# The first cross-attention rewritten: 32-column products, splits on ScalarE and GpSimd, a new order of work in each tile

## What is computed

```python
q = layernorm(x)                         # rows of 512, mean and variance of each
# B = 8 batches, channels 256, length 512, 8 heads of 32 channels
qk  = einsum('bhdq,bhdl->bhql', qh, kh) / sqrt(32)
sm  = softmax(qk, axis=-1)
ret = einsum('bhql,bhdl->bhdq', sm, vh)
x   = x + gamma * ret                    # k and v are both ctx
```

## Time and profile before

| what | value |
|---|---|
| median of three executions | 2164.12 us (2162.57 to 2165.21) |
| the profiled execution: its own time | 2165.63 us |
| the profiled execution: its span | 2163.8 us |
| first masked product of tile 0, of tile 15 | 45.38 us, 489.10 us |
| first instruction of VectorE in the next block | 526.78 us |
| mean granted TensorE clock | 0.957 |

### The profile page before, as it was taken

One profiled execution on the slowest core, in us unless ns is written; L12 is line 12 of the kernel. 1 busy time (PEld: TensorE's weight loads), 2 busy tenths in 40 slices (PEclk: granted clock), 3 DMA queues, 4 the chain that ended last, 5 costly groups with the idle time before them and its releaser, 6 DMA issues. The chain is left out here.

```text
span 2163.8 us, 33174 instructions
## 1 busy us (share of the span) xinstructions
PE 1887.0 (87%) x10911; PEld 876.8 (41%) x11054; DVE 1692.2 (78%) x3042; ACT 1262.2 (58%) x2016; POOL 794.7 (37%) x681
## 2 busy tenths in 40 slices
PE   3998888896699999799398999999999997869998
PEld 0433333332244443354253444444444443324444
DVE  6799999998826637388688999999999994684443
ACT  2666666654534625144146999999999994521211
POOL 3112222212514515000202888888888883000000
PEclk9999999998899999899698999999999998889999
DMA  6754334402000000110001555555555656000000
GB/s 136 231 115 87 72 67 84 84 9 81 0 0 1 0 0 1 65 33 29 25 0 40 108 108 104 108 108 108 108 105 109 108 106 219 5 1 20 20 20 20
DMA packets 343369, 143.06 MB, mean 66 GB/s; under 512 B 307408, under 2 KB 315600, under 8 KB 342096
## 3 DMA queue, kind: packets, MB, share of 16 engines
q1 hardware_dynamic: 343248, 141.51, 29.5%
HBM read 70.15 MB, written 4.19 MB: 34 GB/s over the span
## 5 line engine op out<-in xcount | busy, mean ns | idle before, releaser
L1385 ACT ACTIVATE a_prob<-a_psS,a_bias,q_scale 128x1024 uint8<-128x1024 f32 x512 | 610.6, 1209 | 26.6 <-PE a_psS L1278 25.6
L1314 DVE TENSOR_REDUCE a_tops<-a_psM 128x1 f32<-128x512 f32 x1024 | 622.7, 681 | 2.0 <-PE a_psM L1268 0.4
L1364 POOL CAST a_wide<-a_pairs 128x2048 int16<-128x2048 uint8 x256 | 481.0, 1894 | 97.3 <-DMA a_pairs<-a_prob 84.8
L1268 PE MATMUL a_psM<-KT,QO 128*128 128x512 bf16 x968 | 353.5, 387 | 16.0 <-DVE a_tops L1314 10.3
L1278 PE MATMUL a_psS<-KT,QO 128*128 128x512 bf16 x967 | 292.9, 380 | 6.6 <-ACT a_prob L1385 3.6
L561 PE MATMUL psO<-prob,vs 128*128 128x512 f32 x512 | 267.2, 604 | 25.3 <-ACT prob L361 20.6
L1290 PEld LDWEIGHTS a_psO<-V,a_wide 128*128 128x128 f16 x4096 | 175.3, 96 | 144.3 <-DVE QO L1327 23.0
L361 ACT ACTIVATE prob<-psT 128x512 f32<-128x512 f32 x256 | 150.7, 595 | 127.1 <-PE psT L549 113.4
L675 POOL TENSOR_TENSOR g_sum<-g_sum 128x512 f32<-128x512 f32 x88 | 126.9, 1442 | 196.9 <-DVE g_sum L740 196.9
L1290 PE MATMUL a_psO<-V,a_wide 128*128 128x32 bf16 x4096 | 181.3, 177 | 20.3 <-DVE QO L1327 15.6
L849 PE MATMUL g_psY<-raw_dn,g_hT 128*128 128x512 f32 x352 | 162.2, 622 | 26.2 <-DVE raw_dn L700 15.8
(11 more groups left out here) (194 smaller groups left out, 2892.4 us busy)
## 6 DMA issues: line engine op xcount, KB each, us to landing
xs<-in_x SPq DMA_DIRECT2D x64, 256.0 KB, 4.7
cs<-in_ctx SPq DMA_DIRECT2D x64, 256.0 KB, 7.7
KT<-in_w SPq DMA_DIRECT2D x2, 4096.0 KB, 21.0
raw_gu<-in_gu SPq DMA_DIRECT2D x4, 1408.0 KB, 17.4
vs<-in_ctxT SPq DMA_DIRECT2D x64, 64.0 KB, 2.2
k_cT<-in_ctxT SPq DMA_DIRECT2D x16, 256.0 KB, 2.7
a_pairs<-a_prob SPq DMA_TRANSPOSE x256, 2.7
out<-x_sb SPq DMA_DIRECT2D x16, 256.0 KB, 2.0
```

What stands on the lines that cost most here:

```text
L1268: pe.matmul(psM[n % NM][:, :], QOf[:, i * P:(i + 1) * P], KTf[:, keys:keys + 512], start=True, stop=True).then_inc(shown, 1)
L1314: v.reduce_max(tops[i // JOIN % NB][:, i % JOIN, c:c + 1], psM[n % NM][:, :], AX.X).then_inc(topped, 1)
L1364: pool.tensor_copy(wide[i % NV][:, :, :, :].rearrange("p k c q -> p k (c q)"), both).then_inc(widened, 1)
L1385: act.activation(prob[i % NP][:, k * HK:(k + 1) * HK], psS[g % NS][:, :], ACT.Exp, scale=q_scale[:, i:i + 1], bias=bias[i // JOIN % NB][:, ...
```

## The change

`mix_rows` is written anew, with nothing else touched.

- **Weighing** goes from one fp32 product of 128 stationary columns per unit to two of 32: for each chunk c, four products (one for each head) into partitions 32h to 32h + 31 of `psO` with the head's 32 rows of ctx, then four into the same partitions of a new bank `psE` with ones. A tile has 32 of them, in four bursts. `collect` is then two reads of 128 partitions for a tile in place of eight of 32. `prob` is a ring of 8. ctx for weighing is fetched in one transfer without the ones.
- **Masking**: the maxima's parts of all units stand in one tile of 51 rows (`PARTS`), turned by one transpose and copied once. In `tscore` the product of L549 becomes four products of 128 columns, each with its own 51-row stationary from the constant `less`, which is built once at the start.
- **Splits**: the queries' normalisation goes from VectorE to ScalarE (`normalise`, four of 128x512), and both operands are split the same way: ScalarE masks two halves (`cut_keys`, `cut_queries`, 128x1024 each), GpSimd subtracts head by head. The Newton step, and the second and third part of the maxima, go to GpSimd, as short instructions.
- **Order**: in a tile TensorE issues two `score` of j + 1 after each of the first eight `tscore` (n = 0 to 7, before 6 to 13). VectorE does the 16 maxima of j + 1 first, with nothing between, then the inversions of j - 1, the row copy of j + 1, and last the statistics of j + 3. ScalarE does the start of the roots of j + 3 after its last exponential. `psS` has three banks, the operands three buffers, everything is prepared a tile earlier (`LEAD = 3`), and the hardware loops are unrolled. Half of the decoding of the FP4 weights comes a tile earlier on VectorE.

The diff, cut to its core:

```diff
-    FIRST = 6
     NU = HT * LC
+    RING = 2 * HT
+    NP1 = NU + 1
+    PARTS = 3 * NP1
+    LEAD = 3
...
+        psS = [pb(f"psS{i}", [P, DM], F32) for i in range(3)]
         psT = [pb(f"psT{i}", [P, DM], F32) for i in range(2)]
...
-        psM = pb("psM", [3, NU, P], BF16)
...
+        psO, psE = pb("psO", [P, DM], F32), pb("psE", [P, DM], F32)
+        psM = pb("psM", [PARTS, P], BF16)
...
+        def turns(steps):
+            for j in range(-LEAD, NT):
+                steps(j)
...
+            for j in range(NT):
+                if has(j + 3):
+                    fetch_x(j + 3)
+                if has(j + 2):
+                    fetch_c(j + 2)
+                if has(j + 1):
+                    fetch_v(j + 1)
+                if j == 0:
+                    sp.dma_start(x_sb[:, 0:2, :], x_tiles[:, 0:2, :]).then_inc(x_loaded, 16)
+                if j == 1:
+                    sp.dma_start(x_sb[:, 2:, :], x_tiles[:, 2:, :]).then_inc(x_rest, 16)
+                if 2 <= j < 2 + CH:
+                    g = j - 2
+                    sp.dma_start(env["raw_gu"][:, g, :],
+                                 gu_in[g * P:(g + 1) * P, :]).then_inc(env["gu_loaded"][g], 16)
...
+                own = Counter(pool, root_own, 6 * j)
+                if j:
+                    pool.wait_ge(normed, j)
+                pool.wait_ge(varied, HT * (j + 1))
+                own.link(pool.tensor_scalar(ve[:, :], mv[b][:, :, 1], LN_EPS, None, ALU.add))
+                pool.wait_ge(guessed, j + 1)
+                own.link(pool.tensor_tensor(tmp[:, :], guess[b][:, :], guess[b][:, :], ALU.mult))
+                own.link(pool.tensor_tensor(tmp[:, :], tmp[:, :], ve[:, :], ALU.mult))
+                own.link(pool.tensor_scalar(tmp[:, :], tmp[:, :], -0.5, 1.5, ALU.mult, ALU.add))
+                if j >= 2:
+                    pool.wait_ge(normal, HT * (j - 1))
+                own.link(pool.tensor_tensor(ys[b][:, :], guess[b][:, :], tmp[:, :], ALU.mult))
+                own.link(pool.tensor_tensor(moved[:, :], mv[b][:, :, 0], ys[b][:, :], ALU.mult))
+                pool.tensor_scalar(away[b][:, :], moved[:, :], -1.0, None, ALU.mult).then_inc(normed, 1)
...
+            def keys(j):
+                if j >= 3:
+                    pool.wait_ge(tscored, NU * (j - 2))
+                for h in range(HT):
+                    pool.wait_ge(k_cut, 2 * j + h // 2 + 1)
+                    pool.tensor_tensor(ks[j % 3][:, h, :], cs[j % 2][:, h, :], k_sub[:, h, :],
+                                       ALU.subtract).then_inc(k_ready, 1)
+            def queries(j):
+                if j >= 3:
+                    pool.wait_ge(tscored, NU * (j - 2))
+                for h in range(HT):
+                    pool.wait_ge(q_cut, 2 * j + h // 2 + 1)
+                    pool.tensor_tensor(qs[j % 3][:, h, :], xs[j % 3][:, h, :], q_sub[:, h, :],
+                                       ALU.subtract).then_inc(q_ready, 1)
+            def split(j):
+                b = j % 2
+                own = Counter(pool, part_own, 2 * j)
+                if j:
+                    pool.wait_ge(parts_ready, j)
+                pool.wait_ge(part_hi, j + 1)
+                own.link(pool.tensor_tensor(rrest[:, :], rmax[b][:, 0:NU], rparts[b][:, 0, 0:NU], ALU.subtract))
+                own.link(pool.tensor_copy(rparts[b][:, 1, 0:NU], rrest[:, :]))
+                pool.tensor_tensor(rparts[b][:, 2, 0:NU], rrest[:, :], rparts[b][:, 1, 0:NU],
+                                   ALU.subtract).then_inc(parts_ready, 1)
...
+            def steps(j):
+                if has(j - 2):
+                    finish(j - 2)
+                if has(j + 2):
+                    keys(j + 2)
+                if has(j + 1):
+                    split(j + 1)
+                if has(j + 2):
+                    queries(j + 2)
+                if has(j + 3):
+                    roots(j + 3)
...
+                act.activation(k_sub[:, half, :], cs[j % 2][:, half, :], ACT.Copy,
+                               scale=k_lo[:, :]).then_inc(k_cut, 1)
...
+            def normalise(j, h):
+                if h == 0:
+                    act.wait_ge(normed, j + 1)
+                act.activation(xs[j % 3][:, h, :], xs[j % 3][:, h, :], ACT.Identity, scale=ys[j % 2][:, h:h + 1],
+                               bias=away[j % 2][:, h:h + 1]).then_inc(normal, 1)
+            def cut_queries(j, k):
+                half = slice(2 * k, 2 * k + 2)
+                act.wait_ge(normal, HT * j + 2 * k + 2)
+                if j:
+                    act.wait_ge(q_ready, HT * (j - 1) + 2 * k + 2)
+                act.activation(q_sub[:, half, :], xs[j % 3][:, half, :], ACT.Copy,
+                               scale=q_lo[:, :]).then_inc(q_cut, 1)
...
+            def collect(j):
+                b = j % 2
+                act.wait_ge(pv_done, NU * (j + 1))
+                if j >= 2:
+                    act.wait_ge(mixed_s, j - 1)
+                    act.wait_ge(added, j - 1)
+                act.activation(weighed[b][:, :], psO[:, :], ACT.Copy, scale=gamma[:, :]).then_inc(o_read, 1)
+                act.activation(e_sums[b][:, :], psE[:, :], ACT.Copy).then_inc(o_read, 1)
+            def steps(j):
                 for n in range(NU):
...
+                    if has(j):
+                        exp(j, n)
+                    if n in (0, 1) and has(j + 2):
+                        cut_keys(j + 2, n)
+                    if n == HT - 1 and has(j - 1):
+                        collect(j - 1)
+                    if n == NU - 1 and has(j + 3):
+                        roots(j + 3)
+                    if 6 <= n < 6 + HT and has(j + 2):
+                        normalise(j + 2, n - 6)
+                    if n in (10, 11) and has(j + 2):
+                        cut_queries(j + 2, n - 10)
...
+            def steps(j):
+                if has(j + 1):
+                    maxima(j + 1)
+                if has(j - 1):
+                    invert(j - 1)
+                if has(j + 1):
+                    maxima_rows(j + 1)
+                if has(j + 3):
+                    statistics(j + 3)
+                if has(j - 2):
+                    after(j - 2)
+                if j == NT - 2:
+                    move(0)
+                    move(1)
+                    mask(0)
+                    mask(1)
+                if j == NT - 1:
+                    move(2)
+                    move(3)
+                    scale(0)
+                    scale(1)
+                    mask(2)
+                    mask(3)
+                    scale(2)
+                    scale(3)
...
+            def tscore(j, n):
+                c, h = n // HT, n % HT
+                g = NU * j + n
+                if g >= 2:
+                    pe.wait_ge(exped, g - 1)
+                out = psT[n % 2]
+                pe.matmul(out[:, :], ks[j % 3][:, h, c * P:(c + 1) * P], qs[j % 3][:, h, :],
+                          start=True, stop=False)
                 if n == 0:
...
+                    pe.wait_ge(mrow_ready, j + 1)
+                for q in range(LC):
+                    mm = pe.matmul(out[:, q * P:(q + 1) * P], less[:, h * LC + q, :], mrow[j % 2][:, :],
+                                   start=False, stop=(q == LC - 1))
+                mm.then_inc(tscored, 1)
...
+            def weigh(j, c):
                 if c == 0:
...
+                    pe.wait_ge(v_in_s[j % 2], 16 * (j // 2 + 1))
+                    if j:
+                        pe.wait_ge(o_read, 2 * j)
+                pe.wait_ge(exped, NU * j + HT * (c + 1))
+                for h in range(HT):
+                    pe.matmul(psO[h * D0:(h + 1) * D0, :], vs[j % 2][:, c, h * D0:(h + 1) * D0],
+                              prob[:, (c * HT + h) % RING, :], start=(c == 0), stop=(c == LC - 1))
+                for h in range(HT):
+                    pe.matmul(psE[h * D0:(h + 1) * D0, :], env["ones_f"][:, 0:D0],
+                              prob[:, (c * HT + h) % RING, :], start=(c == 0),
+                              stop=(c == LC - 1)).then_inc(pv_done, 1)
...
+                pe.transpose(psM[:, :], rparts[j % 2][:, :, :].rearrange("p a b -> p (a b)"), id_b[:, :]).then_inc(turned, 1)
...
+            def steps(j):
                 for n in range(NU):
...
+                    if has(j):
+                        tscore(j, n)
+                    if has(j + 1) and n < NU // 2:
+                        score(j + 1, 2 * n)
+                        score(j + 1, 2 * n + 1)
+                    if has(j) and n > 1 and n % HT == 1:
+                        weigh(j, n // HT - 1)
+                if has(j + 1):
+                    turn_maxima(j + 1)
+                if has(j):
+                    weigh(j, LC - 1)
```

More of the change, by code:

```diff
@@ L348, in _ @@
+            def steps(j):
[9 more added lines that the diff above has]
+                    roots(j + 3)
+            turns(steps)
+            finish(NT - 2)
+            finish(NT - 1)
         @block.scalar
@@ L410, in _ @@
```

(70 more changed lines are left out.)

361 lines of the change are left out of this document (124 added, 237 removed).

## The result

The changed kernel takes 2074.04 us (2073.07 to 2076.6) where the kernel before, beside it, takes 2164.43: a ratio of 0.9585, 95% interval 0.9569 to 0.9602. The profiled execution took 2074.52, its span is 2072.8.

The account below looks back on a forecast made before the run. VectorE was taken to set the 29.58 us tile, TensorE following near. From 2165.6, 9.4 at the start, 71.7 in 15 tiles (period 24.8) and 1 at the end leave 2083.5 us, 2082 as median; range 2045 to 2225.

Parts of the forecast that it names:

- The price that decides: Weighing on TensorE: 32 fp32 products of 32 columns overlap by column place, 1.8 us a burst of eight, 7.3 a tile.
- Rival 1: Weighing bursts: fp32 halves start in order, so heads overlap only by half; burst 3.85 us, about 2203 us; chance 0.28.
- Rival 2: Weighing bursts: each 32-column product costs a full 0.86 us, burst 6.9, period 44.5, about 2390 us; chance 0.16.
- Changes of shape: TensorE, between products of different rows or columns: 42 changes a tile at 0.09 us each, 3.8 us.
- Rival 3: TensorE: shape changes cost 0.19 us each with full overlap, period 27.3, about 2120 us; inside the forecast's 0.54.
- Waits of TensorE: In each tile, for late ScalarE exponentials: 0.9 us at the last burst and 2.3 more, 3.2 in sum.
- Start, tiles, end: Gains before tile 0's first masked product, over 15 tiles, and from tile 15's to the next block: 9.4, 71.7, 1 us.
- Transfers: DMA through the tiles: share rises from 0.40 to 0.48, costed at nothing with a tile of lead as cover.
- What is late next: After the change, TensorE (period 24.8 us) and ScalarE (chain 22 to 23) together are late in a tile.
- Rival 4: Shape changes free, TensorE quick: ScalarE's chain holds the period at 23.1, about 2058 us; inside the forecast's 0.54.

Follow-up runs that it names:

- head-by-head kernel: The changed kernel with each head's psO and psE products next to each other in a burst, both in the same place; 2074.34 us, ratio 0.9586 to the kernel before.
- one place: The changed kernel with all 32-column products writing the same 32 partitions, heads added up; 2400.1 us, ratio 1.1089 to the kernel before.

## Why the prediction was right, step by step

- **The price that decides** was taken at the right end: burst 1.8, measured 1.86. It was a choice by plausibility, and to that extent luck: what decided it, that products in different places do not wait for each other, no row before showed.
- **Rival 1, overlap by half**, falls: its first step, starts in order, is refuted by the head-by-head kernel. Its price was sound: a burst of 3.53 gave 2183, where I had 2203 for 3.85. **Rival 2, no overlap**, at 2390, is what one place gives: 2400.
- **Changes of shape**: 0.09 each taken, 0.105 measured for the 32 of the masked products, 3.4 us a tile. Those of the bursts are in the 1.86 and have no price of their own. Rival 3's 0.19 was an fp32 weight load's, and did not carry over. TensorE's issue is 16 x 0.65 + 16 x 0.22 + 4 x 1.86 and the transpose's 0.2, 21.6 as predicted.
- **Waits of TensorE**: 3.2 predicted, 24.2 - 21.6 = 2.6 as a mean, and 23.6 - 21.6 = 2.0 in a steady tile. This is the largest error of the sum. It was halved by what the prediction has no term for: tile 0's 6.9 us at the low clock and behind a transfer, and 1.6 us of low clock in each of two others. In those two TensorE had waited 0.81 us just before, as it does in the tiles where the clock stays; why it fell there is open.
- **ScalarE**: 17.5 predicted. By the groups it is 300.8/16 = 18.8 us of instructions a tile; I priced the normalising by the exponential from a PSUM bank (0.60) and the halves at 1.0. Both were too low: 0.81 and 1.14. From one start to the next they are shorter, 0.70 and 1.04, since neighbours overlap, and the busy time of the tile above is 16.9. The Trainium skill ("ScalarE: Activation LUTs", What ACT_TABLE_LOAD costs) gives 186 ns and 0.833 ns an element, and 93 ns for each scale or bias taken from a tile. That makes 0.80 and 1.13, which the trace bears out; the term could have been had from it. The error cost nothing here, as ScalarE's load was not the bound.
- **GpSimd**: 14.6 predicted, 13.3 in the tile above; the short instructions are 0.20 to 0.23, not 0.3. **VectorE**: 18.0 predicted, 16.7 in the tile above, mostly the maxima at 156.0/16 = 9.75 and the inversions at 54.1/16 = 3.4.
- **Start, tiles, end**, by the prediction's own marks, the first masked products of tiles 0 and 15 (now at 34.89 and 400.51): start 9.4 predicted, 45.38 - 34.89 = 10.5 measured; 15 tiles 71.7 and 78.1; end 1 and 37.7 - 34.4 = 3.3. The key halves begin at 15.71, where I had 15.5; the maxima last 9.65 us in place of 11.0.
- **Transfers**: the share rose to 0.48, as worked out. They were costed at nothing, and from 100 us on no engine waits for one; but ScalarE waits 2.93 us for ctx in tile 0.
- **What is late next**: "TensorE and ScalarE together" was half right. TensorE's issue and ScalarE's order are what later edits moved, by 22 and 12 us. ScalarE's load, which I counted, held nothing, and the wait for the statistics, foreseen at 2.5 and measured at 2.6, is worth 0.02 us in a steady tile. Rival 4's 2058, for free changes of shape, was near: 2051.65 with 32 of 42 gone. Its reason was not: ScalarE's chain was to hold the period at 23.1, and the steady steps go down to 22.64, and to 21.60 with ScalarE's work the same and its halves later.
- The sum gave 2083.5 for the profiled execution, 2074.52 came: 9 us too high, 6.4 of it in the tiles, 2.3 at the end and 1.1 at the start, less 0.9 that the code behind took longer.

The experiments also give a better kernel than either: full rows, statistics ahead, query halves two units later, 2039.33 us, 5.8% below before, where the change is 4.15% below.

## What to carry to other kernels

Products that fill only a part of the stationary's columns are best given different column places and issued in one burst; narrowness alone bought nothing here, places nearly a factor of four. A short contraction is cheaper filled up with zeros where it alternates with full ones, as each change of shape cost half of a 16-bit product here. When the engine that was the bound has been relieved, look at what stands just ahead of the instruction for which another engine waits, not at each engine's sum: two ScalarE instructions moved by two places brought 12 us, four of 0.81 us a tile moved off the engine nothing that the runs can tell. Look at single steps before a mean over tiles is explained: here the first tile alone is 6.9 us longer than its neighbours, and one edit gained its 2.7 us there.

## What the runs showed of the hardware that was not expected

- Four fp32 products of 32 columns in four places pass in 0.89 us (one place: 3.46 to 3.53), and start out of their written order across places.
- Each change between 128 and 51 rows cost 0.105 us on 16-bit products.
- A TensorE that waits 1 to 2 us and then works in short pieces at each tile's start fell near the lower clock (0.56 over 7.65 us of the tile shown; 0.88 over all 15); 2.6 us of products a tile without use in that gap gave 21 us back.
